# First layer of a four-layer kernel: projection and convolution as one set of products, the output bias on POOL, the first pair's decay factors in SBUF

## The reference

```
h = layernorm(x);  h = h * rsqrt(mean(h*h) + eps) * rms_w
x1, g = split(h @ in_W + in_b)                 # 256 channels each
x1 = silu(conv(x1) + conv_b)                   # 4 taps over time, each channel by itself, zeros ahead
delta, B, C = split(x1 @ dbc_W + dbc_b)        # 16 + 16 + 16
delta = softplus(delta @ dup_W + dup_b)
for n in 16 states:  s[t] = exp(delta[t] * A[n]) * s[t-1] + delta[t] * B[t, n] * x1[t]
y = silu(g) * sum over n of s[t] * C[t, n]
x = x + layernorm(x) + y @ out_W + out_b
```

## Time and profile before

| | |
|---|---|
| median of 3 runs | 1689.86 us (1680.04, 1689.86, 1689.9) |
| profiled execution | 1679.67 us, its span 1677.9 us |
| busy over the whole span | PE 1386.4, DVE 1273.9, ACT 1110.4, POOL 862.2 us |
| granted TensorE clock | 0.853 of full speed |

### The profile page before, as it was taken

The page is one execution under the profiler, slowest core; times in us unless marked ns, Lnnn a source line. Parts: engine busy times, 40 slices in busy tenths (PEclk is TensorE's granted clock), DMA queues, the critical chain, the costliest instruction groups (busy, mean ns, idle before and its releaser), DMA issues. The chain is left out here.

```text
span 1677.9 us, 21483 instructions
## 1 busy us (share of the span) xinstructions
PE 1386.4 (83%) x6448; PEld 673.7 (40%) x6448; DVE 1273.9 (76%) x2157; ACT 1110.4 (66%) x1610; POOL 862.2 (51%) x1035
## 2 busy tenths in 40 slices
PE   4788888888888758999999468877788749999998
PEld 3344444444444323444444123333333314444443
DVE  2888787878778986788887488888888528888775
ACT  4766666655656634555555189999999945555554
POOL 5777666667666654555555433232323005555555
PEclk8989787877879988999999566778867669999999
DMA  6121111122111103322222000000000004322241
GB/s 211 64 89 51 50 51 50 52 67 83 50 50 50 51 0 136 151 119 101 101 101 101 0 1 1 0 0 0 0 0 0 1 30 173 114 107 107 111 165 53
DMA packets 27779, 110.88 MB, mean 66 GB/s; under 512 B 4033, under 2 KB 9554, under 8 KB 19282
## 3 DMA queue, kind: packets, MB, share of 16 engines
q1 hardware_dynamic: 27010, 110.15, 17.4%
q10 hardware_dynamic: 720, 0.15, 0.0%
HBM read 107.41 MB, written 2.88 MB: 66 GB/s over the span
## 5 line engine op out<-in xcount | busy, mean ns | idle before, releaser
L828 POOL TENSOR_TENSOR e_h_lo<-e_h,e_h_hi 128x512 f16<-128x512 f32 x272 | 315.0, 1158 | 272.4 <-ACT e_h_hi L944 261.3
L261 POOL TENSOR_TENSOR m_h<-m_b_sb,m_dx 128x512 f32<-128x512 f32 x256 | 319.6, 1271 | 177.4 <-POOLq L67 99.8
L631 DVE TENSOR_TENSOR_SCAN m_h<-m_decay,m_h 128x1024 f32<-128x1024 f32 x128 | 292.5, 2285 | 32.2 <-ACT m_decay L496 19.2
L360 PE MATMUL m_y_ps<-m_hc,ident 128*128 128x512 f32 x512 | 283.2, 681 | 0.0
L496 ACT ACTIVATE m_decay<-m_delta,mw_a_log 128x255 f32<-128x255 f32 x512 | 211.7, 461 | 83.4 <-DVEq L636 83.1
L1039 DVE TENSOR_TENSOR e_cu<-e_u,e_c_bc 128x512 f32<-128x512 f32 x256 | 176.0, 687 | 107.6 <-PE e_u L868 87.0
L939 ACT ACTIVATE e_g<-e_g 128x512 f32<-128x512 f32 x256 | 149.1, 582 | 163.2 <-PE e_g L868 163.2
L868 PE MATMUL e_g<-e_x_hi,ew_gate_up 128*128 128x512 f16 x544 | 210.4, 387 | 8.4 <-ACTq L943 8.4
L1444 DVE TENSOR_SCALAR a_d<-a_s 128x512 f32<-128x512 f32 x256 | 170.2, 686 | 56.7 <-PE a_s L1278 37.6
L868 PE MATMUL e_u<-e_x_hi,ew_gate_up 128*128 128x512 f16 x544 | 209.4, 385 | 0.0
L875 PE MATMUL e_y<-e_h_hi,ew_down 128*128 128x512 f16 x544 | 206.9, 381 | 1.6 <-POOL e_h_lo L828 1.6
(11 more groups left out here) (182 smaller groups left out, 2022.8 us busy)
## 6 DMA issues: line engine op xcount, KB each, us to landing
e_c_bc<-mix SPq DMA_DIRECT2D x64, 1024.0 KB, 6.7
m_b_sb<-b_rows SPq DMA_DIRECT2D x64, 512.0 KB, 5.4
ew_gate_up<-w_gate_up SPq DMA_DIRECT2D x1, 2176.0 KB, 13.5
out<-x_sb SPq DMA_DIRECT2D x8, 256.0 KB, 2.3
ew_down<-w_down SPq DMA_DIRECT2D x1, 1088.0 KB, 11.4
mix<-e_cT SPq DMA_DIRECT2D x16, 32.0 KB, 1.6
x_sb<-x SPq DMA_DIRECT2D x1, 256.0 KB, 2.9
mw_in_w<-w_in_w SPq DMA_DIRECT2D x1, 256.0 KB
```

The costliest lines, as they stand in the source:

```text
L261: ins = nc.gpsimd.tensor_tensor(h[:, m % 4, :, c], b_sb[:, p, 2 * m:2 * m + 2], dx[:, p, c:c + 1].to_broadcast([P, 2, T]), ALU.mult)
L360: ins = nc.tensor.matmul(y_ps[:], ident[:], hc[:, m % 2, n].rearrange("p c t -> p (c t)"), start=(m == 0 and n == 0), stop=(m == PAIRS - 1 ...
L631: nc.vector.tensor_tensor_scan(flat, decay[m % 2][:], flat, 0.0, ALU.mult, ALU.add).then_inc(scan_chain, 1)
L828: nc.gpsimd.tensor_tensor(h_lo[:, k], h[:, k], h_hi[:, k], ALU.subtract).then_inc(h_lo_ready, 1)
```

## The change

**Projection and convolution.** The weights `in_w` for x are multiplied, per tap, by that tap's coefficients (`conv_rows`, a row of 5 x 256 numbers loaded to all 128 partitions), into `taps`. The products with `taps` then read the normalised input `hT`, now with three zero columns ahead of it, and give the convolved projection at once: per chunk four products over shifted columns. The projection's bias becomes a constant per channel (`x_bias`), except in the first three columns; a product of three rows and three columns with `ncorr` corrects these. `project_x`, its copy with bias `pad_x` and `xpad` are gone. The halves of the convolution stand in iterations 2 and 3.

**Output bias.** The two products with a row of ones in `project_out` are gone; `add_bias` on POOL adds `out_b` to a batch's rows of `x_sb` beforehand, in iteration 7, three batches ahead, and `update` waits for it.

**Decay factors.** Pair 0 has a buffer of its own in SBUF, `decay_head`; the other seven alternate between the PSUM tiles. ACT makes pair 0's factors in iteration 6, ahead of the SiLU block, those of pair 1 in iteration 7, behind it, and none in iteration 1. `read_dbc` moves from iteration 1 to 2.

**End.** The epilogue's `halves` instruction is cut in three, with `gate_y` and `update` between.

The diff, cut to its core:

```diff
-        hT = sb("hT", [P, 2, T])
-        xpad = sb("xpad", [P, DC, KC - 1 + T])
-        taps = sb("taps", [P, DC, KC, P])
+        hT = sb("hT", [P, 2, KC - 1 + T])
+        taps = sb("taps", [P, KC, DI])
+        early = sb("early", [KC - 1, KC])
+        ncorr = sb("ncorr", [KC - 1, DI])
+        x_bias = sb("x_bias", [P, 2, DC])
...
+        decay_head = sb("decay_head", [P, 2 * DC * T])
...
+        def decay_of(m, p):
+
+            return decay_head if m == 0 else decay[(m + p) % 2]
...
+            def add_bias(b):
+                take(pool, res_ready)
+                own = x_sb[:, bass.ds(b * TT, TT), :]
+                nc.gpsimd.tensor_tensor(own, own, out_b[:].rearrange("p (o d) -> p o d", o=1).to_broadcast([P, TT, DM]), ALU.add).then_inc(own_ready, 1)
...
+                add_bias(0)
+                add_bias(1)
...
+                    if m == 4 and first:
+                        add_bias(b + 2)
+                    if m == 7 and further:
+                        add_bias(b + 3)
...
-            def project_x(p, bank=t1):
-                take(pe, hT_ready)
-                for c in range(DC):
-                    ins = nc.tensor.matmul(bank[:, c * T:(c + 1) * T], in_w[:, c * P:(c + 1) * P], hT[:, p], start=True, stop=True)
-                ins.then_inc(x1_ready, 1)
...
-            def convolve(c, bank=t1):
+            def convolve(c, p, bank=t1):
                 if c == 0:
-                    take(pe, xpad_ready)
+                    take(pe, hT_ready)
                 for k in range(KC):
-                    ins = nc.tensor.matmul(bank[:, c * T:(c + 1) * T], taps[:, c, k], xpad[:, c, k:k + T], start=(k == 0), stop=(k == KC - 1))
+                    nc.tensor.matmul(bank[:, c * T:(c + 1) * T], taps[:, k, c * P:(c + 1) * P], hT[:, p, k:k + T], start=(k == 0), stop=False)
+                ins = nc.tensor.matmul(bank[:, c * T:c * T + KC - 1], ncorr[:, c * P:(c + 1) * P], ident[0:KC - 1, 0:KC - 1], start=False, stop=True)
...
-                        nc.tensor.matmul(t2[:, tt * DM:(tt + 1) * DM], yg[:, c, tt * P:(tt + 1) * P], out_w[:, c], start=(c == 0), stop=False)
-                    ins = nc.tensor.matmul(t2[:, tt * DM:(tt + 1) * DM], ones[:], out_b[0:1, :], start=False, stop=True)
+                        ins = nc.tensor.matmul(t2[:, tt * DM:(tt + 1) * DM], yg[:, c, tt * P:(tt + 1) * P], out_w[:, c], start=(c == 0), stop=(c == DC - 1))
...
-                project_x(0)
-                pe.sem_inc(z_read, 1)
-                project_g(0)
                 take(pe, zeros_made)
                 take(pe, taps_made)
                 for c in range(DC):
-                    convolve(c)
+                    convolve(c, 0)
+                pe.sem_inc(z_read, 1)
+                project_g(0)
                 transpose_z(y_ps)
                 project_dbc(0)
...
-                    if m == 4 and ahead:
-                        if first:
-                            convolve(0)
-                        convolve(1)
...
-                    if m == (2 if first else 1) and ahead:
-                        project_x(p)
-                    if m == 3 and ahead and not first:
-                        convolve(0)
+                    if m == (3 if first else 2) and ahead:
+                        convolve(0, p)
+                    if m == 3 and ahead:
+                        convolve(1, p)
...
-                    ins = nc.scalar.activation(xs[:, p, c], bank[:, c * T:(c + 1) * T], ACT.Silu, bias=conv_b[:, c:c + 1])
+                    ins = nc.scalar.activation(xs[:, p, c], bank[:, c * T:(c + 1) * T], ACT.Silu, bias=x_bias[:, 1, c:c + 1])
...
-                        ins = nc.scalar.activation(decay[m % 2][:, at + 1:at + T], delta[:, p, c, 1:T], ACT.Exp,
+                        ins = nc.scalar.activation(decay_of(m, p)[:, at + 1:at + T], delta[:, p, c, 1:T], ACT.Exp,
...
+                decays(1, 0)
             def body(b, p, first=False, further=True, ahead=True, last=False):
                 for m in range(PAIRS):
-                    if m < PAIRS - 1 or not last:
+                    if m == 0:
+                        scanned.wait(-1, first)
+                        decays(2, p)
+                    elif 2 <= m < PAIRS - 1:
                         scanned.wait(m - 1, first)
-                    if m == PAIRS - 1 and not last:
+                        decays(m + 1, p)
+                    elif m == PAIRS - 1 and not last:
+                        scanned.wait(m - 1, first)
+                        decays(1, 1 - p)
+                    if m == PAIRS - 2 and not last:
                         take(act, delta_ready)
                         decays(0, 1 - p)
-                    elif m < PAIRS - 1:
-                        decays(m + 1, p)
                     if m == 0 and first:
                         silu_x(1 - p, y_ps)
                         exp_table()
-                    if m == (2 if first else 1) and not last:
+                    if m == 2 and not last:
                         read_dbc(1 - p)
                     if m == 2 and first:
                         normalise(b + 2)
                     if m == (4 if first else 3) and ahead:
                         scale_hT(p)
-                    if m == 4 and ahead and not first:
-                        pad_x()
                     if m == 4 and not last:
                         softplus()
-                    if m == 5 and first:
-                        pad_x()
...
-                for c in range(DC):
-                    for k in range(KC):
-                        ins = nc.vector.tensor_scalar(taps[:, c, k], ident[:], conv_w[:, c, k:k + 1], None, ALU.mult)
-                ins.then_inc(taps_made, 1)
+                row = [conv_rows[:, k * DI:(k + 1) * DI] for k in range(KC + 1)]
+                for k in range(KC):
+                    nc.vector.tensor_tensor(taps[:, k], in_w[:, 0:DI], row[k], ALU.mult)
+                take(dve, early_made)
+                c = Chain(dve, dve_chain)
+                c.link(nc.vector.tensor_scalar(ncorr[:], row[0][0:KC - 1], early[:, 0:1], None, ALU.mult))
+                c.link(nc.vector.scalar_tensor_tensor(ncorr[:], row[1][0:KC - 1], early[:, 1:2], ncorr[:], ALU.mult, ALU.add))
+                c.link(nc.vector.scalar_tensor_tensor(ncorr[:], row[2][0:KC - 1], early[:, 2:3], ncorr[:], ALU.mult, ALU.add))
+                nc.vector.tensor_tensor(ncorr[:], ncorr[:], row[KC][0:KC - 1], ALU.mult).then_inc(taps_made, 1)
+                c.link(nc.vector.tensor_reduce(x_bias[:, 0], conv_w[:], AX.X, ALU.add))
+                c.link(nc.vector.tensor_tensor(x_bias[:, 0], x_bias[:, 0], in_b[:, 0:DC], ALU.mult))
+                nc.vector.tensor_tensor(x_bias[:, 1], x_bias[:, 0], conv_b[:], ALU.add).then_inc(bias_made, 1)
...
-                    nc.vector.tensor_tensor_scan(flat, decay[m % 2][:], flat, 0.0, ALU.mult, ALU.add).then_inc(scan_chain, 1)
+                    nc.vector.tensor_tensor_scan(flat, decay_of(m, p)[:], flat, 0.0, ALU.mult, ALU.add).then_inc(scan_chain, 1)
...
-                gate_y((NB - 1) % 2)
                 take(dve, upper["dve"])
                 raw, halves = ew.parts[0]
-                nc.vector.scalar_tensor_tensor(halves[1][:], raw[:], W_SCALE, halves[0][:], ALU.mult, ALU.subtract)
-                update(NB - 1)
+                for e in range(0, NE + 1, 6):
+                    if e == 6:
+                        gate_y((NB - 1) % 2)
+                    if e == 12:
+                        update(NB - 1)
+                    some = slice(e, min(e + 6, NE + 1))
+                    nc.vector.scalar_tensor_tensor(halves[1][:, some], raw[:, some], W_SCALE, halves[0][:, some], ALU.mult, ALU.subtract)
...
+                  "conv_rows": [P, (KC + 1) * DI], "out_w": [P, DC, DM], "out_b": [P, DM]}
+                 w[n].to_broadcast([P, (KC + 1) * DI]) if n == "conv_rows" else w[n]) for n in self.NAMES]
+        "conv_rows": np.concatenate([a["conv_w"].T.reshape(1, -1), a["in_b"][:DI].reshape(1, -1)], 1),
```

More of the change, by code:

```diff
@@ L111, in sem @@
             return sems.enter_context(nc.semaphore("m_" + name))
-        in_w, in_b, rms_w, conv_w, conv_b, neg_a, dbc_w, dbc_b, dup_w, out_w, out_b = (mw.sb[n] for n in mw.NAMES)
+        in_w, in_b, rms_w, conv_w, conv_b, neg_a, dbc_w, dbc_b, dup_w, conv_rows, out_w, out_b = (mw.sb[n] for n in mw.NAMES)
         pick = sb("pick", [96, 2 * NS, P], FP16)
-        ones = sb("ones", [1, P])
         konst = sb("konst", [P, 4, TT])
@@ L153, in mamba_layer @@
         z_ready, zT_ready, hT_ready = sem("z_ready"), sem("zT_ready"), sem("hT_ready")
-        x1_ready, g_ready, xpad_ready, conv_ready, xs_ready = (sem(n) for n in ("x1_ready", "g_ready", "xpad_ready", "conv_ready", "xs_ready"))
+        g_ready, conv_ready, xs_ready = (sem(n) for n in ("g_ready", "conv_ready", "xs_ready"))
         dbc_ready, bcd_ready, bc_hi_ready, bc_ready = (sem(n) for n in ("dbc_ready", "bcd_ready", "bc_hi_ready", "bc_ready"))
@@ L217, in zeros @@
                 nc.gpsimd.memset(bc[:], 0.0)
```

(37 more changed lines are left out.)

7 lines of the change are left out of this document (2 added, 5 removed).

## The result

The changed kernel takes 1592.46 us (four runs, 1592.23 to 1594.22), the kernel before on the same chip 1689.88: a ratio of 0.9444, 95% interval 0.9404 to 0.9484. One of the four runs of the kernel before took 6905.62 us and is not in the ratio. Forecast were 1628 and a range from 1600 to 1656; it is 7.5 us faster than the range's low end. The profiled execution took 1592.62 us, its span is 1590.9, 87.0 less than before.

The account below looks back on a forecast made before the run. First-layer batches: DVE's work plus its waits for TensorE and ScalarE. Waits -87.3, left or new +21, lock +4, start +5: -57, giving 1622.7 from the profiled execution or 1632.9 from the median; forecast 1628, range 1600 to 1656.

Parts of the forecast that it names:

- Which low stretch?: TensorE's clock in the first layer's batches: 7 us low in every batch, leaving 1.5 us of DVE waits each.
- Waits of 87.3 us removed: DVE's waits over 14 first-layer batches for C, decay factors, make_delta and update all go: -87.3 us.
- 21 us left or new: DVE waits for C and make_delta remaining in the 14 batches, 1.5 us each: +21 us.
- The floor of 30.4 us: First-layer batch without the four waits: 36.64 - 6.24 = 30.4 us, DVE's 29.8 busy plus the 0.5 chain.
- The lock, 4 us: Scan 0 and POOL instructions, all reading SBUF, exclude each other: DVE loses 0.25 us a batch, POOL 2.2; +4 us, at most 19.
- Start, +5: Layer's start: conv_rows load, later statistics and SiLU, two add_bias and lock, less one projection: +5 us, between +1 and +9.
- End, 0: Layer's end: update goes before the last third of halves, but POOL still excludes DVE: 0, from -2 to +2.
- The second, no waits left: First-layer batches: no DVE waits left at all, 21 us less, 1607 us; chance 12%.
- Rival 1: TensorE's clock: the old alternation of low stretches stays, 2.85 us of waits a batch, 1647 us; chance 20%.
- Rival 3: Scan 0 against POOL inputs: the lock costs 2.0 us a batch instead of 0.25, 1654 us; chance 11%.
- Rival 4: TensorE idles more around the batch's end, clock low through most of a batch: slower than before, up to 1880; chance 3%.
- Rival 5: TensorE stays the bound, only half of ScalarE's wait goes: -15 us with the start's +5, 1677 us; chance 4%.

Follow-up runs that it names:

- head buffer alone: Kernel before with only pair 0's decay factors in their own SBUF buffer, made ahead of the SiLU block: 1644.0 us, ratio 0.982.
- filler: Kernel before plus seven matrix products a batch on TensorE, results unread, in its idle stretch around a batch's end: 1626.8 us, ratio 0.972.
- bias alone: Kernel before with only the output bias added by POOL instead of by TensorE products: 1630.0 us, ratio 0.974.
- without the head buffer: Changed kernel with decay factors as before, all in PSUM and pair 0 behind the SiLU block: 1596.7 us, ratio 0.955.

## Why the prediction was wrong

**The step that failed** is "Which low stretch?", where I took "7 us, as in the batch of 0.90, for every batch", and from it 1.5 us of waits a batch, 21 us. The profile after has 0 to 3.6 us of low clock a batch, and in the 14 batches DVE waits for PE not once. The reason I gave for it was wrong in two ways. I let the fall come from ACT's wait passed on to PE; but with the head buffer alone ACT's wait is gone and the clock is still 0.89, and with bias or filler alone the wait stays and the clock is 0.94 or 0.99. And I let the idling shrink to 0.5 us; it is still 1.78 us, the clock falls behind it in some batches and not in others, and is up again sooner.

What the runs show in its place: nearly all of the wait for C was the low clock's doing. Less work for PE in the stretch (bias alone, 42.9 us down to 8.4) and more work for it in the gaps (filler, down to 4.8) both take most of it away. Why the clock falls in one batch and not in the next, why a low stretch lasts 17, 7 or 3.6 us, and why less work shortens it, is open; no run here sets the length of a stretch by itself. A loop is plausible, late PE makes DVE late and DVE PE idle, but it was only argued.

**Term by term**, from the sum's 1622.7 against the profiled execution to its 1592.6:

- Waits of 87.3 us removed: right, all of it. The mechanism named for ACT's 19.2 us was too simple: in the full change the head buffer takes some 4 us, the SiLU block's earlier start the rest (only 3.0 us of ACT's wait come back without the head buffer); alone, it takes them all.
- 21 us left or new: none in the 14 batches, 1.1 in the last. This is 21 of the 30 us missed.
- The floor of 30.4 us: 30.05, and 30.0 without the 0.9 us by which one scan was held, so 6 us in the loop. I took it as the old batch without its waits. But two DVE instructions in a row overlap by 0.08 us (2.28 us long, 2.20 apart), and each of 67 waits had cost this as well, which comes to 5.4.
- The lock, 4 us: POOL's part was sized well, 1.6 us a batch for 2.2. DVE's was not; 0.9 us in 15 batches for 4, all of it in the second scan 0. Later it is nothing, because `add_bias` ends just as scan 0 starts (164.42 + 0.73 = 165.15 against 165.03), and POOL's next input, from 165.41, is the one that waits:

```profile
164.42 0.73 POOL L276 TENSOR_TENSOR x_sb<-x_sb,mw_out_b 128x256 f32 x1
165.41 6.66 POOL L270 TENSOR_TENSOR m_h<-m_b_sb,m_dx 128x512 f32<-128x512 f32 x4 [0.26 <-POOLq L67]
```

  Four inputs of 1.27 are 5.1; the other 1.6 is the scan's. The rule quoted from the Trainium skill (SBUF — State Buffer, SBUF: two separate sides) holds, and by it the side that comes second pays, here POOL.
- Start, +5: 5.15. Its parts differ: 1.84 to the first scan; 1.0 by which that scan is longer and 0.95 by which the second waits longer for POOL, both the lock; 1.4 for the two `add_bias`. The second scan before:

```profile
40.18 2.29 DVE L631 TENSOR_TENSOR_SCAN m_h<-m_decay,m_h 128x1024 f32<-128x1024 f32 x1 [0.22 <-POOL m_h L261]
```

- End, 0: -0.3. Two of the three `halves` pieces run in 1.91 and 1.47 us, the middle one is held by POOL's 5.68 us instruction, as expected:

```profile
524.05 1.91 DVE L666 SCALAR_TENSOR_TENSOR ew_gate_up<-ew_gate_up 128x1536 f16<-128x1536 f32 x1
...
527.07 4.67 DVE L666 SCALAR_TENSOR_TENSOR ew_gate_up<-ew_gate_up 128x1536 f16<-128x1536 f32 x1
```

- The base: 5.3 us of the miss of 35.5 come from setting 1628 between the profiled execution and the median. The changed kernel has no such gap, 1592.6 and 1592.5.

**The rivals.** The second, no waits left, happened; with the floor right it would have said 1601, not 1607. I gave it 12% because "every batch seen has some low stretch". Some still have one; 3.6 us of it simply costs nothing. Rivals 1, 3, 4 and 5 fell: the alternation is gone, scan 0 is held once in the 14 batches, the clock is higher, PE isn't the bound. The range rested on the clock's habits staying, and was too narrow for that. Rival 5's time doesn't follow from its own terms: 15 us off the 1685 from which the forecast counts is 1670, not 1677.

Of the signs named ahead, ACT's wait gone, `make_delta`'s near zero and POOL inputs of up to 3.5 us (3.24) came; about 20 us of waits for C (0.6), batches of 31 to 33 us (29.9 to 30.1) and a first scan 3 us later (1.84) did not.

## What to carry to other kernels

Before waits for TensorE are priced by its work, read the granted clock batch by batch: if waits and low clock go together, put a few unused products into TensorE's gaps as a probe, and if the kernel gets faster the clock was the cause. The worth of one part of a change then depends on the others, since any part that brings the clock back takes most of those waits. A batch less its waits was 6 us too high here as a floor; check it against the distance between instructions that don't wait.

## What was not expected of the hardware

- More matrix work made the kernel faster: 22 us more of PE busy time in 400 us, 47 us less in all (1674.1 to 1626.8), with the granted clock up from 0.83 to 0.99.
- The same idling of 1.78 us (and 0.37) was followed by some 7 us of low clock in one kernel, by 3.6 in another, and by none at all in other batches of that same kernel.
- The kernel with long low stretches scatters (1661 to 1690 us, up to 26 between runs on one chip); the changed one, without them, lies within 0.2%.
- A scan of 1024 columns takes 2.28 us with its factors in PSUM and in SBUF alike; from SBUF it makes a POOL instruction beside it up to 2 us longer.
